# The causal mask of an attention stage moved into the score products, with the maxima turned one unit earlier and the first value product one unit later

## The reference, cut to what matters

```
x = x + 0.5 * ffn(layernorm(x))      # top-1 of 8 experts, hidden width 512
x = x + attn(layernorm(x))
x = x + 0.5 * ffn(layernorm(x))

def attn(x):
    xn = x * rsqrt(mean(x * x) + EPS) * norm_w
    q, k, v = (heads(xn @ W.T + b) ...)              # 16 heads of 8
    scores = q @ k.T * scale
    causal = triu(ones(T, T), k=1)
    scores = where(causal, -inf, scores)
    attn = softmax(scores)
    return xn + (attn @ v) @ Wo.T + bo
```

## Time and profile before

| | us |
|---|---|
| median of 3 runs | 322.96 (321.8 to 323.7) |
| span of the profiled execution, first to last instruction | 319.3 |
| median less this span | 3.7 |
| PE busy | 276.5 (87%) |
| DVE busy | 214.5 (67%) |
| POOL busy | 178.8 (56%) |
| ACT busy | 159.7 (50%) |

### The profile page before, as it was taken

One profiled execution on the slowest core, in us unless ns is written; L12 is line 12 of the kernel. 1 busy time (PEld: TensorE's weight loads), 2 busy tenths in 40 slices (PEclk: granted clock), 3 DMA queues, 4 the chain that ended last, 5 costly groups with the idle time before them and its releaser, 6 DMA issues.

```text
span 319.3 us, 7990 instructions
## 1 busy us (share of the span) xinstructions
PE 276.5 (87%) x2396; PEld 224.1 (70%) x2396; DVE 214.5 (67%) x691; ACT 159.7 (50%) x389; POOL 178.8 (56%) x319
## 2 busy tenths in 40 slices
PE   8573999999995776999999999998977699999960
PEld 8463999999994363656666566665646588999960
DVE  3877048788608759987666777776787555888850
ACT  2430076666204834586666667768541107666620
POOL 5577815554525201587777787788657730554551
PEclk9855999999999998799999999999976579999996
DMA  6973141220040731662524522110001143222100
GB/s 180 403 293 119 53 95 54 65 63 31 24 126 8 199 121 53 197 180 88 156 79 134 152 72 74 57 53 6 3 19 42 42 121 86 51 67 71 34 10 0
DMA packets 34387, 29.37 MB, mean 92 GB/s; under 512 B 4108, under 2 KB 28817, under 8 KB 34352
## 3 DMA queue, kind: packets, MB, share of 16 engines
q1 hardware_dynamic: 29696, 23.52, 24.6%
q0 software_dynamic: 2496, 4.27, 4.1%
q10 hardware_dynamic: 2160, 1.14, 1.4%
HBM read 17.08 MB, written 12.55 MB: 93 GB/s over the span
## 4 chain that ended last, share of the span: by engine, by line
PE 58%; POOL 11%; DVE 10%; issue 7%; DMA 5%; ACT 4%; POOLq 1%; ACTq 0%; SPq 0%; DVEq 0%
PE bank L1279 13%; PE bank L1290 12%; PE bank L1207 5%; PE bank L1436 3%; PE bank L1408 3%; PE bank L1384 3%; POOL pT L541 2%; POOL row L454 2%; PE bank L1381 2%; PE bank L1414 2%; PE bank L1271 2%; POOL disp_d L462 2%; PE bank L1240 2%; PE bank L1466 2%; PE bank L1389 1%
## 5 line engine op out<-in xcount | busy, mean ns | idle before, releaser
L723 ACT ACTIVATE pT<-bank 128x512 f32<-128x512 f32 x96 | 56.4, 599 | 36.2 <-PE bank L1414 25.2
L1207 PE MATMUL bank<-zero 128*128 128x128 f32 x298 | 43.2, 314 | 9.4 <-DVE rowi L916 4.7
L1279 PE MATMUL bank<-xsT,ew 128*128 128x128 f32 x368 | 48.8, 276 | 0.2
L1290 PE MATMUL bank<-experts,hT 128*128 x368 | 48.9, 276 | 0.0
L1207 PEld LDWEIGHTS bank<-zero 128*128 128x128 f32 x298 | 41.6, 227 | 10.1 <-DVE rowi L916 4.7
L1038 DVE TENSOR_REDUCE mh<-bank 128x2 f32<-128x512 f32 x64 | 42.1, 682 | 8.5 <-PE bank L1384 8.2
L541 POOL TENSOR_SCALAR_AFFINE_SELECT pT<-pT 128x512 f32<-128x512 f32 x62 | 39.8, 643 | 10.2 <-ACT pT L723 9.9
L1279 PEld LDWEIGHTS bank<-xsT,ew 128*128 128x128 f32 x368 | 44.7, 192 | 0.7 <-ACT xsT L621 0.3
L1290 PEld LDWEIGHTS bank<-experts,hT 128*128 128x128 f32 x368 | 44.8, 192 | 0.5 <-issue 0.3
L627 ACT ACTIVATE hT<-bank,ew 128x128 f32<-128x128 f32 x92 | 28.8, 364 | 28.9 <-PE bank L1279 28.9
L923 DVE TENSOR_SCALAR hT<-bank,ew 128x128 f32<-128x128 f32 x92 | 28.0, 346 | 20.2 <-PE bank L1279 18.9
(11 more groups left out here) (133 smaller groups left out, 479.4 us busy)
## 6 DMA issues: line engine op xcount, KB each, us to landing
sp_d<-spl SPq DMA_DIRECT2D x32, 192.0 KB, 2.6
experts<-in_experts SPq DMA_DIRECT2D x8, 578.0 KB
qz<-sp_d SPq DMA_DIRECT2D x32, 96.0 KB
ks<-sp_d SPq DMA_DIRECT2D x32, 96.0 KB
xs_sb<-disp_d SPq DMA_DIRECT2D x46, 66.0 KB, 1.8
row<-in_x SPq DMA_DIRECT2D x4, 256.0 KB, 5.5
row<-x_d SPq DMA_DIRECT2D x4, 256.0 KB, 5.0
disp_d<-pad ACTq DMA_DIRECT2D x12, 66.0 KB, 2.3
```

The lines of the kernel that those rows point to most:

```text
L723: act.activation(pT[:, u, :], bank[2 + u % 2][:, :], ACT.Exp, scale=SCALE).then_inc(a_e, 1)
L1207: pe.matmul(bank[b][:, 0:P], zero[:, :], zero[:, :], start=True, stop=True)
L1279: mm = pe.matmul(bank[2 + 2 * (k % 2) + c // 2][:, (c % 2) * P:(c % 2 + 1) * P], ew[:, k % WRING, c * P:(c + 1) * P], xsT[:, k % 2, :], st ...
L1290: mm = pe.matmul(bank[6 + k % 2][:, 0:D], hT[:, k % 2, c, :], w2.rearrange("p a c -> p (a c)"), start=(c == 0), stop=(c == HC - 1))
```

## The change

The mask becomes part of the products. Each head now has its own stack of 128 rows in both `qz` and `ks`: 48 rows of parts, three for the maxima (rows 48 to 50), and from row 63 rows of a table (`stack_rows`, a new input `tri`) whose products are hugely negative where a key lies behind the query's block of two. Every unit of scores_q and scores_k becomes four products of 128 columns, one per head and quarter; a product that needs no mask contracts 65 rows, the others 128. The identity products, POOL's masks and DVE's last two masks are gone. The table is loaded once and copied into the buffers by ACT (three times 128 x 4096 bf16) and POOL (once); the memsets of the stacks and the table `low` are gone. As scores_q now reads the rows of the maxima too, SP first writes zeros into them at each reload of a stack, a fifth transfer. Two moves: `max_copy` and `turn_max` stand behind unit 1 instead of unit 2, and `pv(half, 0)` behind unit 5 instead of unit 4, except in sequence 7.

```diff
-SROWS = 2 * JROWS
+SROWS = BLK * HD
+TROW = 65
...
                 need(sp, a_st, 12 * (b - 2) + 6 * half + 6)
+                if not isinstance(b, int) or b >= 2:
+                    sp.dma_start(qz[k][MROW:KROWS, half, :, :, :].rearrange("s j i n -> s (j i) n"),
+                                 zero[MROW:KROWS, :].bitcast(BF16).unsqueeze(1).broadcast_to((3, 8, T))
+                                 ).then_inc(a_stk[k][half], 16)
...
-                pool.memset(qz[k][:, :, :, :, :].rearrange("p h j i n -> p (h j i n)").bitcast(F32), 0.0
-                            ).then_inc(static_s, 1)
+                pool.wait_ge(tri_s, 16)
+                pool.tensor_copy(qz[k][:, :, :, :, :].rearrange("p h j i n -> p (h j i) n"),
+                                 tri[:, 0:T].unsqueeze(1).broadcast_to((P, NH, T))).then_inc(static_s, 1)
...
-                for n in range(4 if more or half == 0 else 2):
-                    mask(b, half, n // 2, n % 2)
+                for n in range(4):
...
             route_exp(0, 1)
+            stack_fill(qz[0], 0)
             route_exp(0, 2)
+            stack_fill(ks[0], 1)
             pad_rows(0, range(NE))
+            stack_fill(ks[1], 1)
             expert_tiles(0)
...
                     exp_unit(b, half, u)
-                    if u == 2:
+                    if u == 1:
                         if half == 0:
                             max_copy(b, 1)
...
-            last_mask(2)
             add_out(6)
-            last_mask(3)
...
                 o = bank[u % 2]
-                if w < 2:
-                    pair = 4 * half + 2 * pp + w
-                    ov = o[:, :].rearrange("p (j n) -> p j n", j=2)
-                    pe.matmul(ov[:, :, P:T], ident_b, maskS.unsqueeze(1).broadcast_to((P, 2, P)),
-                              start=True, stop=False, **MM_BANK)
-                    for j in range(2):
-                        mm = pe.matmul(ov[:, j, :], qz[k][0:SROWS, half, j, pair - 4 * half, P:T],
-                                       ks[k][0:SROWS, pair, :],
-                                       start=False, stop=True, **MM_BANK)
...
+                ov = o[:, :].rearrange("p (h n) -> p h n", h=4)
+                for h in range(4):
+                    if w < 2:
+                        i, j, late, kt, rows_ = 2 * pp + w, h // 2, 1, h % 2, P if h % 2 else TROW
+                    else:
+                        i, j, late, kt, rows_ = 2 * pp + h // 2, h % 2, 0, 0, P
+                    mm = pe.matmul(ov[:, h, :], qz[k][0:rows_, half, j, i, late * P:(late + 1) * P],
+                                   ks[k][0:rows_, half, j, i, kt * P:(kt + 1) * P],
+                                   start=True, stop=True, **MM_BANK)
...
-                pe.wait_ge(a_pm, 8 * b + 4 * half + 2 * pp + 2)
+                pe.wait_ge(a_e, 12 * b + 6 * half + 3 * pp + 3)
...
-                    if u == 2:
+                    if u == 1:
...
-                    if u == 4:
+                    if u == 4 and not more:
+                        pv(b, k, half, 0)
+                    if half == 0 and not first and u == 4:
+                        need(pe, a_x, b - 1)
+                        turn_out(b - 1, 0)
+                    if u == 5 and more:
                         pv(b, k, half, 0)
```

More of the change, by code:

```diff
@@ L99, in constants, with stack_rows, build @@
     return c
-def build(nc, x_in, wqkvo, cols_in, rows_in, w_gate, experts_in, const_in, out):
+def stack_rows():
+    c = np.zeros((P, 2, T), np.float32)
+    c[MROW:KROWS, 1, :] = -1
+    t = np.arange(T)
+    for row, block, half in ([(TROW - 2, P // 2 - 1, 0), (TROW - 1, P // 2 - 1, 1)]
+                             + [(TROW + r, r, None) for r in range(P // 2 - 1)]):
+        here = np.ones(T, bool) if half is None else t // P == half
+        n = t % P
+        last = block == P // 2 - 1
+        c[row, 0, here & (n == 2 * block)] = 2.0 ** UP
+        if not last:
+            c[row, 0, here & (n == 2 * block + 1)] = 2.0 ** DOWN
+        c[row, 1, here & (n == 2 * block + 1)] = -2.0 ** NEXT
+        c[row, 1, here & (n > 2 * block + 1)] = -2.0 ** FAR
+    return c.reshape(P, 2 * T)
+def build(nc, x_in, wqkvo, cols_in, rows_in, w_gate, experts_in, const_in, tri_in, out):
     ctx = ExitStack()
@@ L193, in build @@
         qz = [sb(f"qz{i}", [P, 2, 2, 4, T], BF16) for i in range(2)]
-        ks = [sb(f"ks{i}", [P, NPAIR, T], BF16) for i in range(2)]
+        ks = [sb(f"ks{i}", [P, 2, 2, 4, T], BF16) for i in range(2)]
+        tri = sb("tri", [P, 2 * T])
         mh = sb("mh", [P, 2, 2, 2, 4])
@@ L479, in _ @@
                 ln_scale(0, q)
[L480 to L483, removed]
             pool.wait_ge(ids_s, 1)
@@ L527, in max_split @@
                 pool.tensor_tensor(s_[:, :, 2, :], r_, z_, ALU.add).then_inc(a_mb, 1)
[L529 to L542, removed]
             def step(b, half, more=True):
@@ L645, in expert_tiles, with stack_fill @@
                     step(t, t, do_T=t + 2 < NS, do_h=t + 1 < NS)
+            def stack_fill(buf, which):
+                act.wait_ge(tri_s, 16)
+                act.copy(buf[:, :, :, :, :].rearrange("p h j i n -> p (h j i) n"),
+                         tri[:, which * T:(which + 1) * T].unsqueeze(1).broadcast_to((P, NH, T))
+                         ).then_inc(static_s, 1)
             act.dma_start(wg[:, :], w_gate).then_inc(gate_s, 16)
@@ L1374, in scores_q @@
                 if u == 0:
[L1375 removed]
+                    pe.wait_ge(a_stk[k][half], 80 * bh + 64)
                 need(pe, a_mx, 12 * b + 6 * half + u - 1)
                 o = bank[u % 2]
[L1378 to L1395 removed]
+                ov = o[:, :].rearrange("p (h n) -> p h n", h=4)
[7 more added lines that the diff above has]
+                                   start=True, stop=True, **MM_BANK)
                 mm.then_inc(a_s, 1)
@@ L1404, in scores_k @@
                 o = bank[2 + u % 2]
[L1405 to L1416 removed]
+                ov = o[:, :].rearrange("p (h n) -> p h n", h=4)
+                for h in range(4):
+                    if w < 2:
+                        i, j, late, qt, rows_ = 2 * pp + w, h // 2, 0, h % 2, TROW if h % 2 else P
+                    else:
+                        i, j, late, qt, rows_ = 2 * pp + h // 2, h % 2, 1, 1, P
+                    mm = pe.matmul(ov[:, h, :], ks[k][0:rows_, half, j, i, late * P:(late + 1) * P],
+                                   qz[k][0:rows_, half, j, i, qt * P:(qt + 1) * P],
+                                   start=True, stop=True, **MM_BANK)
                 mm.then_inc(a_st, 1)
             def pv(b, k, half, pp):
[L1422 removed]
+                pe.wait_ge(a_e, 12 * b + 6 * half + 3 * pp + 3)
                 if pp == 0:
@@ L1578, in _ @@
             expert_tiles(1)
-_INS = ["x", "wqkvo", "cols", "rows", "w_gate", "experts", "const"]
+_INS = ["x", "wqkvo", "cols", "rows", "w_gate", "experts", "const", "tri"]
 def kernel(L0_attn_x, L0_attn_norm_w, L0_attn_Wq, L0_attn_bq, L0_attn_Wk, L0_attn_bk, L0_attn_Wv, L0_attn_bv,
@@ L1604 @@
         "const": constants(),
+        "tri": stack_rows(),
     }
```

70 lines of the change are left out of this document (13 added, 57 removed).

## The result

The changed kernel took 319.91 us (median of 14 runs, 318.55 to 321.46), the kernel before 322.75 (14 runs, 320.8 to 324.88). The ratio is 0.9913, with a 95% interval of 0.9891 to 0.9934: faster by 0.9%, or 2.8 us, where 6.1 were forecast. The profiled execution of the changed kernel took 320.33 us, with a span of 318.5 against 319.3.

What follows compares the result with a forecast made beforehand. The prediction took PE to issue nearly all the time, with ScalarE's copy chain just beneath. Gains of 2.2 + 0.9 + 1.1 + 0.5 + 1.4 = 6.1 us gave 316.9 us, range 311 to 321.5 (forecast's own 314 to 319.5).

Steps and rivals of the forecast that it cites:

- SP is the bound: Attention: maxima rows landing more than 0.5 us late keep halves near 6.6 us; time 320 us, chance 0.08.
- (a): Sequences 1 to 4 of attention: each 0.55 us shorter, 2.2 us in all.
- (c): Sequence 0, partly at the low clock: 1.1 of 1.8 us of masks gained.
- the layout of half 1: Steady half 1, from its k0: project at 4.68 us behind ACT's copies, the half ending at 6.46 against 6.56.
- Half 0, laid out at 6.32: Steady half 0, from its k0: turn_out can start at 4.14 us, the half ending at 6.32 against 6.77.
- SP's fifth transfer: Stack reloads: five transfers take 3.8 us behind k5; maxima rows may go 0.3 late, some 3.4 us left until k0.
- Costs put at nothing: ACT's fills (at most 4.2 us each), POOL's fill (about 5 us), the table's load and SP's added transfer: no cost.
- (e): Sequence 7: 0.6 of DVE's 2.08 us wait gained, and 0.8 from removing DVE's last mask; 1.4 us.
- The 3.7 us: Whole kernel: the runs' median stands 3.7 us above the 319.3 us span, carried over unchanged.
- The waits stay: Attention: PE's issue plus today's 1 us of waits gives 11.5 us a sequence; time about 309 us, chance 0.16.
- Weight loads bind: Score units: eight loads in a row slow the matmuls; about 325.5 us at 0.08 pitch, near 339 at 0.108; chance 0.11.
- The clock drops again: Attention: PE idles more; one more low-clock stretch costs 1.2 to 2 us, two bring 320.5; chance 0.12.

Runs made afterwards that it cites:

- the clearing on GpSimd: Changed kernel with the zeroing transfer for the stacks' maxima rows issued by GpSimd behind its split instead of by SP; 319.03 us, ratio to before 0.9904.
- the clock held: Changed kernel with 14 idle TensorE products added in the first query scores, before sequence 0; 318.75 us, ratio to before 0.9881.
- ScalarE's order: Changed kernel with ScalarE copying oT (half 0) and anT (half 1) ahead of the fourth exponential; 317.74 us, ratio to before 0.9888.
- the value product back: Changed kernel with only the first value product of each half moved back behind the fifth unit; 319.39 us, ratio to before 0.9892.
- two together: Changed kernel with the zeroing transfer on GpSimd and ScalarE's output copies ahead of the fourth exponential; 314.72 us, ratio to before 0.9752.
- the fastest version: Changed kernel with the zeroing transfer on GpSimd, ScalarE's output copies earlier and SP's four stores spread over two halves; 313.53 us, ratio to before 0.9698.
- the old masks under the new orders: Kernel before, old masks kept, with both moves, ScalarE's output copies earlier and SP's stores spread; 327.59 us, ratio to before 1.0137.

## Why the prediction was right and wrong

- **Direction and mechanism** held: faster, with PE's waits ahead of turn_out (0.28) and project (0.78), released by oT and anT. The late value product does uncover ScalarE's chain. 319.91 lies in the range of 311 to 321.5, but outside the forecast's own 314 to 319.5. It is the figure that I gave for *SP is the bound* (320), and that is chance: no k0 of the changed kernel from 150 to 222 us is in the list of PE's waits.
- **What failed is the sum, terms (a) and (c).** (a) gave 4 x 0.55 = 2.2 us and measured 0.4; (c) gave 1.1 and measured 0.3. The other terms came to 3.1 against 2.8 forecast. So the stages of the two profiles gained 3.8 us where 6.1 were summed; the medians show 2.8 (2.1 to 3.5 by the interval), and where the last 1.0 went stays open, since what lies ahead of the first q differs by more than that between profiles.
- **The step in (a): the layout of half 1, 6.46 us.** In sequences 2 to 4 half 1 measured 6.66, 6.66 and 6.67. The layout let k3 follow k2 and q2 directly. In the rows after, turn_norm stands between q2 and k3 (179.58 and 179.81), so the fourth exponential starts 3.38 behind k0 and not 3.19, project 4.78 and not 4.68, and the value product behind it 0.1 late again. I had counted turn_norm in PE's total and left it out of the chain. Its 0.23 us (179.58 to 179.81) is the larger part; turn_max, priced at 0.11, took 0.21 (178.92 to 179.13) and is the rest. That is 0.6 us over the three sequences. It is read from the rows; no run moved turn_norm. Half 0, laid out at 6.32, measured 6.38, 6.52 and 6.39, another 0.3; in the 6.52 the last turn_out (176.24) is followed by k0 at 176.94 and not after 0.45, 3.27 us behind the issue of the maxima's rows at 173.67, so SP was the later chain there; with the clearing on GpSimd the same half takes 6.32. And the kernel before took 13.27 a sequence in the mean, not the 13.33 of the one I read: 0.2. Together that is the 1.1 us missing in sequences 2 to 4. Sequence 1 adds 0.65: its half 0 took 7.32 us (143.41 to 150.73), with the split late behind the reductions.
- **"SP's fifth transfer", costed at nothing**, held for most halves of the changed kernel, but by less than the 3.4 us I gave it: I took the landing for short, and it takes some 3.2. I also left out the four stores, 2.2 us, which stand ahead of the loads in half 1 of sequences 0 to 3. The rows' issue came 3.25 us behind k0 in half 0 of sequence 3 (173.67), where I had 2.5 to 3.
- **Sequence 0, term (c).** I took 1.1 of 1.8 us of masks without a chain laid out, and 0.3 came. With the clock held it was no shorter, since k0 waited for the rows. What would have to go for the whole 1.1 to arrive stays open.
- **Costs put at nothing** that were nothing. The fills took 3.60 us each on ACT and on POOL; the routing exponential at 22.51 came at 22.47, and ScalarE's first step on an expert tile (xq), at 39.93 before, at 39.91. DVE's wait of 2.08 us in sequence 7 is gone, and the gate logits on PE are next, as said in (e).
- **The 3.7 us** between span and median, carried over unchanged, is no fixed cost: every run's time lies 1.7 to 2.2 us above its own span (320.33 and 318.5 in the changed kernel), and the profile before was a short execution.
- **The rivals.** *The waits stay* didn't come: no order of these kernels ran a sequence in 11.5, the best about 11.9. *Weight loads bind* fell: 0.47 us for eight matmuls is 0.058 each, where four gave 0.056. The Trainium skill (TensorE: Matmul & The Clock Gate, Back-to-back issue gap) gives about 81 ns for a stream of loads and matmuls of 128 columns; the measurement decides, and here it says 58. *The clock drops again* is in the profile (0.55 from 127 to 138 us, has 0.78 over ten), but holding the clock didn't shorten the sequence. *SP is the bound* came true as soon as ScalarE's chain was shortened or hidden again, in three runs (the masks alone, ScalarE's order and, together with GpSimd's split, the value product back).
- **The price I never gave the edit:** it is two edits of opposite sign. The masks alone measured 318.74, the moves alone 331.56. With the new masks the moves cost next to nothing (319.91 against 318.74, within the intervals), because without them SP's queue sets nearly the same pace.

## What to carry to other kernels

When a wait is removed or work taken off the busiest engine, lay out every queue's own sum for one period, DMA issues with the stores between them, before the saving is counted: here three chains (TensorE with ScalarE's copies, GpSimd's split, SP's queue) set nearly the same pace, 12.5 to 13.2 us in sequences 2 to 6 whichever of them bound, and single repairs measured as nothing while two together gave 2.5% and three 3.0%. In a layout by hand, put each instruction in the chain in which it stands, not only in its engine's total. An order that hides one wait is worth testing again after the next edit: the two moves cost 2.5% with the old masks, and next to nothing with the new ones. They are part of the fastest version; whether they help there was not run.

## What the runs showed of the hardware

In the changed kernel's attention an issue holds SP's queue for 0.70 to 0.79 us for 12 KB of rows and for 96 KB of stacks alike, and for 0.36 to 0.53 in most stores of 192 KB: the size doesn't set it. Once a store took 1.61 (at 167.52 in the chain above), which was not looked into. Where a k0 waited for the maxima's rows, it started 2.6 to 3.7 us behind their issue, 3.1 to 3.5 in most cases. On GpSimd the same clearing transfer took 0.58 to 0.74 us to issue and delayed nothing that the waits show. Stretches of low clock ahead of the attention came and went between kernels with the same code there: a granted clock of 0.50 for some 3 to 7 us around 102 us in eleven profiles, and none in three (the kernel before, ScalarE's order, the old masks under the new orders).
